# A graph network's prologue: degree roots on VectorE, variance roots ahead of the tables, the partition maximum by transposes

## The reference, cut to what matters

```
deg  = segment_sum(edge_weight and 1 for the own loop, target)
dis  = where(deg > 0, rsqrt(deg), 0)
norm = dis[row] * edge_weight * dis[col]
h    = layer_norm(...) @ W.T
out  = segment_sum(h[row] * norm, col) + b
xn   = layernorm(x)                      # (x - mean) / sqrt(var + eps)
```

## Time and profile before

| what | before |
|---|---|
| median of three runs | 4391.79 us |
| profiled execution, its own time | 4389.59 us |
| its span | 4387.9 us |
| busy PE, DVE, ACT, POOL | 3602.8, 2497.3, 1195.3, 3105.3 us |
| mean granted TensorE clock | 0.917 of full |

### The profile page before, as it was taken

One profiled execution on the slowest core, in us unless ns is written; L12 is line 12 of the kernel. 1 busy time (PEld: TensorE's weight loads), 2 busy tenths in 40 slices (PEclk: granted clock), 3 DMA queues, 4 the chain that ended last, 5 costly groups with the idle time before them and its releaser, 6 DMA issues.

```text
span 4387.9 us, 93816 instructions
## 1 busy us (share of the span) xinstructions
PE 3602.8 (82%) x26676; PEld 3055.0 (70%) x26677; DVE 2497.3 (57%) x8916; ACT 1195.3 (27%) x3161; POOL 3105.3 (71%) x3378
## 2 busy tenths in 40 slices
PE   5967767767767767767767999999999999999989
PEld 4755556556656655556556888888888887888878
DVE  8855545545455555545554665665666665665655
ACT  2521001001101101001013444444444444444434
POOL 3357777777777777777767777777777777777772
PEclk9988889878888888888888999999999999999999
DMA  4044444444444444444434343443344343444431
GB/s 150 34 135 126 130 119 129 130 119 125 130 123 126 130 122 126 131 119 129 126 110 118 112 117 113 117 118 115 112 118 118 112 117 114 116 117 115 115 110 53
DMA packets 256045, 515.37 MB, mean 117 GB/s; under 512 B 61480, under 2 KB 154032, under 8 KB 255984
## 3 DMA queue, kind: packets, MB, share of 16 engines
q0 software_dynamic: 151392, 413.60, 33.3%
q1 hardware_dynamic: 104592, 101.17, 6.9%
HBM read 474.81 MB, written 39.71 MB: 117 GB/s over the span
## 4 chain that ended last, share of the span: by engine, by line
PE 50%; DVE 15%; issue 11%; POOL 10%; DMA 7%; ACT 4%; DVEq 2%; SPq 1%; POOLq 0%; ACTq 0%
PE bank L1255 48%; POOL gs L558 10%; DMA gr<-h_d,idx_r 7%; DVE ss L1011 2%; PE bank L1277 2%; DVE rstd L755 2%; DVE rstd L753 2%; DVE rstd L754 1%; ACT L734 1%; DVE st L762 1%; ACT bank L734 1%; DVE w L1152 1%; ACT w L737 1%; DVEq L1011 1%; DVE u L771 1%
## 5 line engine op out<-in xcount | busy, mean ns | idle before, releaser
L558 POOL DMA_INDIRECT gs<-h_d,idx_all x3038 | 2901.0, 955 | 956.3 <-issue 640.9
L1255 PE MATMUL bank<-gs,ss 128*128 128x256 f32 x6272 | 1599.2, 402 | 11.5 <-DMA gs<-h_d,idx_all 11.3
L1255 PEld LDWEIGHTS bank<-gs,ss 128*128 128x128 f32 x6272 | 1218.7, 202 | 191.6 <-DMA gs<-h_d,idx_all 21.6
L1011 DVE TENSOR_SCALAR ss<-iw,dst_all,ew 128x128 f32<-128x128 f32 x3152 | 878.6, 350 | 180.0 <-PE bank L1255 122.7
L734 ACT ACTIVATE bank<-bank,eb1c 128x128 f32<-128x128 f32 x1616 | 448.8, 340 | 634.3 <-PE bank L1255 631.9
L1255 PE MATMUL bank<-experts,w 128*128 128x256 f16 x4848 | 604.4, 278 | 17.1 <-DVE w L1152 17.1
L1255 PE MATMUL bank<-w,experts 128*128 128x128 f16 x9696 | 608.3, 219 | 0.0
L1255 PEld LDWEIGHTS bank<-w,experts 128*128 128x128 f16 x9696 | 569.0, 98 | 44.3 <-issue 16.6
L1255 PEld LDWEIGHTS bank<-experts,w 128*128 128x128 f16 x4848 | 467.8, 100 | 91.1 <-issue 22.4
L1255 PE MATMUL bank<-gr,sr 128*128 128x256 f32 x232 | 115.1, 590 | 480.4 <-DMA gr<-h_d,idx_r 480.3
L1152 DVE SCALAR_TENSOR_TENSOR w<-bank,w 128x512 f16<-128x512 f32 x404 | 277.9, 688 | 360.4 <-ACT w L737 359.6
(11 more groups left out here) (271 smaller groups left out, 3443.3 us busy)
## 6 DMA issues: line engine op xcount, KB each, us to landing
gs<-h_d,idx_all POOLq DMA_INDIRECT x3038, 2.7
hself<-h_d SPq DMA_DIRECT2D x100, 128.0 KB, 3.3
ew_in<-in_eW SPq DMA_DIRECT2D x49, 168.0 KB, 2.6
out<-u SPq DMA_DIRECT2D x51, 128.0 KB
u<-xn_d SPq DMA_DIRECT2D x50, 128.0 KB
h_d<-u SPq DMA_DIRECT2D x50, 128.0 KB, 1.9
u<-x_d SPq DMA_DIRECT2D x50, 128.0 KB
u<-r_d SPq DMA_DIRECT2D x50, 128.0 KB
```

The source lines that it names most:

```text
L558: pool.indirect_dma_start(gs[:, n, :], None, table[:, :], bass.IndirectOffsetOnAxis(ap=idx_all[:, w, n:n + 1], axis=0), element_offset=P * ...
L1011: m = dve.tensor_scalar(ss[:, slot + j, :], iw[:, :], dst_f[:, bass.ds(c, 1)], ew[:, bass.ds(c, 1)], ALU.is_equal, ALU.mult)
L1255: return pe.matmul(out_ap, lhsT, rhs, start=first, stop=last, **kw)
```

## The change

Seven things change, all in the prologue.

1. SP loads w6, w7, wk and the layer norm columns first, under a semaphore of their own, `weights_first`; the other 16 loads keep `weights_in`.
2. The maximum over partitions goes over TensorE: one transpose of `range_part` into a bank, a reduction on VectorE, a transpose back into a row. `partition_all_reduce` is gone.
3. GpSimd splits the edge weights right after its first cast, ahead of the casts of node numbers.
4. VectorE does mean, variance and their roots right after `bn_stats`, and the tables after them.
5. The shifts of w6 and w7 and what ScalarE makes of them no longer wait for all weights; the bias and the scaling of w1 come later.
6. GpSimd does no roots. Its degree part is tile 0 and one loop over 24 pairs.
7. VectorE does the roots of the first two parts as 16 single instructions each, one at each of the eight places between the steps of a tile, from tile 30 and from tile 44 on. Its tile loop becomes a loop of five turns, a written-out turn, a loop of one turn, and a written-out turn. ScalarE waits for `dis_set` at each tile that it scales.

GpSimd and its roots (`root`, `root_seed`, `root_step`, `root_end` are deleted whole):

```diff
+            pc.link(pool.tensor_tensor(wide_s, ew[:, :], part[0], ALU.subtract))
+            pc.link(pool.tensor_copy(part[1], wide_s))
+            pc.link(pool.tensor_tensor(wide_s, wide_s, part[1], ALU.subtract))
+            pc.link(pool.tensor_copy(part[2], wide_s))
             pool.wait_ge(s["prep_set"], 2 + Q + 2)
             pool.tensor_copy(own_q, ints_q)
             pool.tensor_copy(own_n, ints_n)
             pc.link(pool.tensor_copy(dst_f[:, :], dst_i))
-            pc.link(pool.tensor_tensor(wide_s, ew[:, :], part[0], ALU.subtract))
-            pc.link(pool.tensor_copy(part[1], wide_s))
-            pc.link(pool.tensor_tensor(wide_s, wide_s, part[1], ALU.subtract))
-            pc.link(pool.tensor_copy(part[2], wide_s))
             assert pc.n == EDGE_LINKS
 
             def degrees_rest(t):
...
-            for i in range(2):
-                with pool.Fori(CUTS[i] // 2 + 2 * min(i, 1), CUTS[i + 1] // 2) as p:
-                    degrees_rest(2 * p + 1)
-                    degrees_rest(2 * p + 2)
-                t = CUTS[i + 1] + 1
-                degrees_rest(t)
-                root_seed(i)
-                degrees_rest(t + 1)
-                root_step(i)
...
+            with pool.Fori(0, (W - 1) // 2) as p:
+                degrees_rest(2 * p + 1)
+                degrees_rest(2 * p + 2)
```

ScalarE:

```diff
                     if scale is not None:
+                        act.wait_ge(s["dis_set"], part)
                         scaled(scale + 2 * b)
                     turned(t + 1)
                     if b == 0 and out is not None:
...
-            act.copy(w1bias[:, :], bank[3][:, 0:HBLK])
             for k in range(KB):
                 act.activation(w6[:, k, :], w6[:, k, :], ACT.Copy, scale=lncol[:, 0, k:k + 1])
-                act.activation(w7[:, k, :], w7[:, k, :], ACT.Copy, scale=lncol[:, 2, k:k + 1])
-                a = act.activation(w1[:, KB + k, :], w1[:, KB + k, :], ACT.Copy, scale=mixcol[:, 0, k:k + 1])
+                a = act.activation(w7[:, k, :], w7[:, k, :], ACT.Copy, scale=lncol[:, 2, k:k + 1])
             a.then_inc(s["weights_set"], 1)
-            act.wait_ge(s["shift_ps"], 4)
+            act.wait_ge(s["shift_ps"], 3)
             act.copy(u8[:, :], wide(2)).then_inc(s["weights_set"], 1)
             act.wait_ge(s["stats_set"], 1)
             xn_tile(0, 0, 0)
             xn_tile(1, 1, 0)
+            act.wait_ge(s["shift_ps"], 4)
+            act.copy(w1bias[:, :], bank[3][:, 0:HBLK])
             turned(0)
+            for k in range(KB):
+                a = act.activation(w1[:, KB + k, :], w1[:, KB + k, :], ACT.Copy, scale=mixcol[:, 0, k:k + 1])
+            a.then_inc(s["weights_set"], 1)
...
             pair(first + 1)
-            act.wait_ge(s["dis_set"], 1)
             with act.Fori(first + 2, second) as p:
                 pair(p, scale=4 * p - 4 * (first + 2))
             n = 4 * (second - first - 2)
             pair(second, scale=n, out=1)
             pair(second + 1, scale=n + 4)
             assert n + 8 == CUTS[1]
-            act.wait_ge(s["dis_set"], 2)
-            pair(second + 2, scale=n + 8)
+            pair(second + 2, scale=n + 8, part=2)
             degrees_out(2)
             key_exp(W - 1)
```

VectorE, the maximum and the new place of the roots of the variance (their code is the same as before):

```diff
 
             dve.wait_ge(s["edges_in"], 16 * 3)
+            dve.wait_ge(s["prep_set"], 2)
             dve.tensor_scalar(ints_q, dst_i, QN.bit_length() - 1, None, ALU.arith_shift_right).then_inc(s["prep_set"], 1)
             dve.tensor_scalar(ints_n, dst_i, QN - 1, None, ALU.bitwise_and).then_inc(s["prep_set"], 1)
+
+            dve.wait_ge(s["range_max"], 1)
+            dve.tensor_reduce(range_top[0:2 * W, :], range_t, AX.X, ALU.max).then_inc(s["range_top"], 1)
...
+            dve.wait_ge(s["bn_all"], W)
...
+            dve.sem_inc(s["stats_set"], 1)
+
+            dve.wait_ge(s["range_max"], 2)
...
             first, last, prev, lo, eq, gap, shared, n_all, n_deg = (row(i) for i in range(9))
-            ch.link(dve.tensor_scalar(first, range_all[0:1, 0:W], -1.0, float(NCH), ALU.mult, ALU.add))
...
```

VectorE, the roots in the tile loop:

```diff
-            with dve.Fori(0, (W - 1) // TURN) as p:
+
+            def root_steps(i):
+
+                v, minus_half, y, w = (a[:, CUTS[i]:CUTS[i + 1]] for a in (deg_w, w_s2, w_s1, w_s3))
+                one = dis[:, 1 + CUTS[i]:1 + CUTS[i + 1]]
+                links = s["root_links"]
+                n = ROOT_LINKS * i
+                dve.wait_ge(s["deg_out"], i + 1)
+                dve.scalar_tensor_tensor(out=v, in0=v, scalar=1.0, in1=deg_x[:, CUTS[i]:CUTS[i + 1]], op0=ALU.add,
+                                         op1=ALU.add).then_inc(links, 1)
+                yield
...
+                for k in range(NEWTON):
+                    dve.wait_ge(links, n + 6 + 3 * k)
+                    dve.tensor_tensor(w, y, y, ALU.mult).then_inc(links, 1)
+                    yield
+                    dve.wait_ge(links, n + 7 + 3 * k)
+                    dve.tensor_tensor(w, w, minus_half, ALU.mult).then_inc(links, 1)
+                    yield
+                    dve.wait_ge(links, n + 8 + 3 * k)
+                    dve.scalar_tensor_tensor(out=y, in0=w, scalar=1.5, in1=y, op0=ALU.add, op1=ALU.mult).then_inc(links, 1)
+                    yield
+                dve.wait_ge(links, n + 6 + 3 * NEWTON)
+                dve.tensor_tensor(one, one, y, ALU.mult).then_inc(s["dis_set"], 1)
+                yield
+
+            def tiles(p, part=None):
+
+                steps = root_steps(part) if part is not None else None
                 lo = own_column(dve, TURN * p + 1)
                 for j in range(TURN):
                     t, b = TURN * p + j, (j + 1) % 2
+
+                    def aside():
+                        if steps is not None and t >= CUTS[part + 1] + 2:
+                            next(steps, None)
+
                     degrees_sum(t, 1 - b)
+                    aside()
                     degrees_quarter(t + 1, lo)
+                    aside()
                     lo_next = degrees_weighted(t + 1, b, lo, t + 2 if j < TURN - 1 else None)
+                    aside()
                     keys(t)
+                    aside()
                     rows_h(t)
+                    aside()
                     key_sum(t)
+                    aside()
                     index_list(t + 1, lo)
+                    aside()
                     degrees_own(t + 1, b)
+                    aside()
                     lo = lo_next
+
+            first, second = -(-CUTS[1] // TURN), -(-CUTS[2] // TURN)
+            assert TURN * first <= CUTS[1] + 2 and TURN * second <= CUTS[2] + 2
+            with dve.Fori(0, first) as p:
+                tiles(p)
+            tiles(first, 0)
+            with dve.Fori(first + 1, second) as p:
+                tiles(p)
+            tiles(second, 1)
+            assert TURN * (second + 1) == W - 1
             degrees_sum(W - 1, 0)
             last_w = slice(CUTS[2], W)
```

TensorE:

```diff
 
 
+            pe.wait_ge(s["prep_set"], 2)
+            pe.transpose(range_t, range_part, ident[:, :]).then_inc(s["range_max"], 1)
+            pe.wait_ge(s["range_top"], 1)
+            pe.transpose(range_row, range_top[0:2 * W, :], ident[0:2 * W, 0:2 * W]).then_inc(s["range_max"], 1)
...
+            pe.wait_ge(s["weights_first"], 16 * FIRST_LOADS)
...
+                mm(wide(5 + k), zero_tile[:, 0:P], zero_tile[:, :], True, True)
+            pe.wait_ge(s["weights_set"], 1)
+            mm(wide(2), ones_row[:, :], hb[:, 0, :], True, True).then_inc(s["shift_ps"], 1)
+
+            pe.wait_ge(s["weights_in"], 16 * WEIGHT_LOADS)
             for j in range(HBLK):
```

More of the change, by code:

```diff
@@ L69 @@
 L1_LINKS = 2 * LN_LINKS + 6
-WEIGHT_LOADS = 20
+FIRST_LOADS = 4
+WEIGHT_LOADS = 16
 LATE = NE // 2
@@ L227, in gps_kernel @@
         ew_parts = tail.take(DCOL * PARTS, BF16).rearrange("p (a c) -> p a c", a=PARTS)
-        range_part, range_all = tail.take(2 * W), tail.take(2 * W)
+        range_part, range_top = tail.take(2 * W), tail.take(1)
         cmin, cmax = tail.take(RB), tail.take(RB)
@@ L301, in _ @@
             n = 0
-            for t, a in ((w6, W6T), (w7, W7T), (wp, WpT), (wq, Wq), (wk, Wk), (wv, Wv), (wm, Wm), (w1, W1), (w2, W2)):
+            for t, a in ((w6, W6T), (w7, W7T), (wk, Wk)):
+                sp.dma_start(t[:, :, :], a.rearrange("(k p) n -> p k n", p=P)).then_inc(s["weights_first"], 16)
+            with nc.allow_non_contiguous_dma(reason="a few columns"):
+                sp.dma_start(lncol[:, :, :], ln_cols).then_inc(s["weights_first"], 16)
+            for t, a in ((wp, WpT), (wq, Wq), (wv, Wv), (wm, Wm), (w1, W1), (w2, W2)):
                 sp.dma_start(t[:, :, :], a.rearrange("(k p) n -> p k n", p=P)).then_inc(s["weights_in"], 16)
@@ L614, in degrees_out, with pair @@
                 act.copy(deg_w[:, CUTS[i]:CUTS[i + 1]], bank[2][:, 0:CUTS[i + 1] - CUTS[i]]).then_inc(s["deg_out"], 1)
-            def pair(p, scale=None, out=None):
+            def pair(p, scale=None, out=None, part=1):
                 for b in (0, 1):
```

(27 more changed lines are left out.)

89 lines of the change are left out of this document (25 added, 64 removed).

## The result

The changed kernel took 4377.87 us (median of 11 runs, 4377.22 to 4379.64), the kernel before on the same chip 4389.05 (11 runs, 4388.32 to 4392.85): a ratio of 0.9974 with a 95% interval of [0.9966, 0.9982]. That is 11.2 us or 0.26% faster, where the forecast had 9.0; the interval stands for 7.9 to 14.9 us. The profiled executions took 4377.28 (span 4375.6) and 4389.59 (span 4387.9).

The account below looks back on a forecast made before the run. TensorE's messages and GpSimd's gathers bound most of the span; only the prologue before the first gather could move. +2.1 - 7.25 - 4.85 + 1.0 = -9.0 us gave a median of 4382.8 (chance 0.55), range 4374 to 4390.

Parts of the forecast that it names:

- rival A: Start: GpSimd and VectorE take no turns, so it gains 5.2 us; -16.3 in all, 4375.5 us; chance 0.17.
- bound of 8.8 us: Whole kernel: 0.2% of the time, about what a measurement can tell from no change; the forecast's spread lies across it.
- The start, +2.1: Prologue before the tiles: GpSimd and VectorE take turns, first transpose at 59.1 instead of 56.97, a loss of 2.1 us.
- The first root, 23.36: Tiles 28 to 34: roots moved off GpSimd shorten the stretch from 30.61 to 23.36 us, a gain of 7.25.
- The second root, 30.70: Tiles 41 to 48: roots moved off GpSimd shorten the stretch from 35.53 to about 30.7 us, a gain of 4.85.
- Fresh code, +1.0: VectorE's entries into new code pieces at tiles 30, 36 and 42: stands costing 1.0 us in all.
- Rival C: VectorE's three entries into fresh code: 6.5 us each, +9.5 in all, slower at 4401.3 us; chance 0.10.
- Rival B: Tile loop: each root step at its dependent price, 3.1 us a root, start +2.9; -4.8, 4387.0 us; chance 0.18.
- `dis_set`, the w1 part, SP's order and the first one-hot row: Prologue: ScalarE's wait for roots, later w1 work, reordered loads and GpSimd's first one-hot row were each taken to cost nothing.
- One to one into the end: From the prologue to the kernel's end: each microsecond before the first gather at 267.12 us moves the end by one.

Follow-up runs that it names:

- splits_late: Changed kernel with GpSimd's four splitting instructions put back behind its casts of node numbers; 6302.46 us, ratio 0.9966 to the kernel before on the same chip.
- steps_block: Changed kernel with all 16 steps of a root in a row at one place of a tile; 6313.57 us, ratio 0.9991 to the kernel before.
- woven: Changed kernel with GpSimd's splits behind its node-number casts, `src_row` loaded behind x, variance-root and table chains interleaved; 4367.24 us, ratio 0.9949 to the kernel before.
- start_only: Changed kernel with GpSimd's roots and VectorE's single tile loop of the kernel before; 6325.03 us, ratio 0.9999 to the kernel before on the same chip.
- before_again: The unchanged kernel before, run once more on another chip for its prologue landmarks; 6334.77 us (one run).

## Why the prediction was right

The forecast held in sign and, for the time, roughly in size (9.0 for 11.2), and its course did: the first gather moved, and the time with it. The close size is in part luck. By its own steps, the first gather should have moved by -9.0 and moved by -13.8, and the loops gave back part of the excess. The time alone doesn't tell the forecast from rival A either: the measured median of 4377.87 lies 4.9 us under the forecast's 4382.8 and 2.4 over A's 4375.5, and at the first gather 13.8 is nearer to A's 16.3 than to 9.0. What tells is the timeline, where the turns stand and the first transpose comes later, not 5.2 us earlier. Nor did the forecast choose a side of its own bound of 8.8 us: it gave faster and same 0.45 each. Where the 4.8 us lie (1.2 in the start, 0.5 and 1.9 in the two roots, 1.0 in fresh code, 0.3 between the roots):

- **The start, +2.1, measured +0.9.** The mechanism was right: turns for whole instructions, a reduction not held. The size was off. I gave each turn its full duration; in the trace each overlaps the one before by 0.14 (0.68 for 0.82, 1.34 for 1.49), and eight turns make 1.1. `bn_stats` starts at 28.68 in place of 30.0, the added reduction took 0.28 where I had 0.3, the tables' first instruction 0.20 as forecast, the first transpose came at 57.85, not 59.1. Splits_late shows that the turns cost 5.8 us: of rival A's 5.2 there were 4.95 to be had (56.97 to 52.02), but not by this change, in which GpSimd wasn't held up: its four instructions run from 13.21 to 24.22.
- The rule of the Trainium skill (SBUF — State Buffer, "Who interferes with whom") holds here in the parts that ran: the products with two SBUF inputs took 3.65 and 1.99 in place of 0.82, and the `tensor_reduce` L760 its plain 0.82 with L485 under way. L761, a `tensor_scalar` with one input, took 2.59 in place of the 0.48 to which splits_late returns it; the rule has such an instruction block in a two-port mode, and the trace doesn't show the mode.
- **The first root, 23.36, measured 22.83.** Tiles 28 to 29 took the 4.17 that were kept, 29 to 31 took 7.88 where I had 8.42, 31 to 34 10.78 for 10.77. A step on 28 columns costs (3.94 - 3.51) / 8 = 0.05 us of a tile, by tile 30 to 31, the one with eight steps, in place of the net 0.09 that I took. In the timeline of VectorE a step lies between two others, 0.08 before its neighbour:

```profile
174.41 0.17 DVE L952 TENSOR_SCALAR w_s<-deg_w 128x28 f32<-128x28 f32 x1
174.49 0.48 DVE L922 SCALAR_TENSOR_TENSOR experts<-bank,rstd_all,u 128x256 f32<-128x256 f32 x1
174.88 0.17 DVE L954 TENSOR_SCALAR w_s<-deg_w 128x28 int32<-128x28 int32 x1
174.96 0.48 DVE L917 SCALAR_TENSOR_TENSOR u<-u,valid 128x256 f32<-128x256 f32 x1
```

- **The second root, 30.70, measured 28.79**, the term that was most off. Tiles 41 to 43 took 8.24 (8.57 kept), tiles 43 to 47 14.46 (15.92), tile 48 6.09 (6.19). I had given this part the same 1.4 as the first and tiles with ScalarE's scaling at 3.63 each; the four took 3.40, 3.79, 3.62 and 3.65, so these steps cost next to nothing. The number of columns isn't the reason: most steps have 0.16 or 0.17 us in VectorE's rows on 14 columns and 0.17 or 0.18 on 28. Why the tiles around tile 44 have room for them no run shows. Besides, 34→41 shrank by 0.3.
- **Fresh code, +1.0, measured 0.** At the entries of after VectorE stands for 0.27 us (tile 30), nothing (36) and 0.58 (42) without a releaser, less than in the one loop of before. Rival C had its price from two stands that belong to other places: that at the window loop is still there (2.42 for 2.48), that of GpSimd is not.
- **Rival B** (dependent step price, 3.1 a root) fell: tiles 29 to 31 took 0.9 over twice 3.51, and the second root less. In steps_block, where the steps do follow each other, the price is paid, and the stretch takes 27.8.
- `dis_set`, the w1 part, SP's order and the first one-hot row cost nothing, as taken: tile 1 follows the first transpose by 13.2 us as before, tiles 1 to 28 take 94.9 (94.8), and tile 48 to the first gather 10.6 in both.
- **One to one into the end** held only in part. 13.8 us at the first gather became 12.3 in the spans and 11.2 in the medians; with woven 10.35 became 9.33. In the traces of before and after the lead is kept through most of the first loop: ScalarE's first `t_a` instruction of a window comes 13.8 us earlier in the first window, 13.9 in the 33rd and 12.9 in the 49th. The errors partly cancel: with all terms of the prologue right I would have forecast 13.8 and been 2.6 too far. Of the 4.9 us between the forecast median of 4382.8 and 4377.87, 2.7 are none of its steps: before's median of 3 runs was 4391.79, that of 11 is 4389.05. Why the loops give back one or two microseconds stays open; no run tested it, and the interval of the ratio would hold 13.8 too.

## What to carry to other kernels

An engine that is only a helper in a dense loop, as GpSimd here, costs the limiter its lateness and can cost it a stretch at the lower clock besides; price such a stand by the distances of undisturbed turns, not by the wait's row. Small steps spread singly between a loaded engine's other instructions cost about 0.05 us each here, in a block several times that. Long work of GpSimd over SBUF (here two subtractions and two casts of 1568 columns) belongs beside `bn_stats` or reductions, not beside VectorE's two-input instructions, and two independent chains of small dependent instructions are worth weaving.

## What the runs showed of the hardware that was not expected

- A stand of TensorE of 2.58 us in the loop was followed by matmuls at the rate of the lower level (1.91 us for what takes 1.03; granted clock 0.50, then 0.83). With the steps in halves (stands of up to 0.99) the clock stayed at 1.00. The length of a stand alone doesn't tell: in before the clock stayed at 1.00 behind one of 2.23 us (to 171.78), and was 0.85 and 0.81 in the two windows from 185 us, around one of 2.21 (to 187.09); in start_only it was 0.77 and 0.89 in the two windows from 170 us, around one of 2.22, and 1.00 in the two from 185, around one of 2.20.
- `bn_stats` beside GpSimd's two-input instructions: neither is slowed. In splits_late L487 takes its plain 3.15 (from 26.07), and `bn_stats` takes 0.33 us each in the first 21 (6.95 from 21.60, so about 13 of them ahead of L487) as in the other 28 (9.25).
- Two engines that take turns overlap by about 0.14 us at each change: L484 ends 1.34 us behind L758 for its 1.49, L759 0.68 behind L484 for its 0.82.
- The same roots on GpSimd made 11.1, 9.2 or 8.5 us of waits, with no change in them, only in what surrounds them.
- The same kernel took 4389, 6254, 6315 and 6325 us by chip, with the prologue the same to 0.3 us. On the slow ones engines stand in the loops over windows with releasers that the profile doesn't name: the chain of before_again gives 37% of the span to "another core or an unknown queue", that of before none. The cause is open.
